# Two-layer graph block: low parts of the scores added behind the attention's trip through DRAM, and one PSUM bank of scores for even and one for odd graphs

## The reference, cut to what matters

```python
def layer(h, params):                       # two layers; h: 128 graphs x 128 nodes x 384
    u = einsum('bid,bjd->bij', h, h) / sqrt(D)
    a = softmax(u, axis=-1)
    delta = a * adjacency_matrix
    attn = delta / (sum(delta, axis=-1, keepdims=True) + 1e-10)
    hl, hs, hr = h @ wl.T + b_l, h @ ws.T + b_s, h @ wr.T + b_r
    ctx = (attn * upper) @ hl + diagonal(attn) * hs + (attn * lower) @ hr
    o = (ctx - mean(ctx)) / sqrt(var(ctx) + 1e-12) * g + beta
    return relu(o)
x = layernorm(x + layer(layer(x)))          # eps 1e-5, over the features
```

## Time and profile before

| | us |
|---|---|
| median of 3 runs (lowest, highest) | 1632.81 (1631.94, 1633.05) |
| the profiled execution's own time | 1631.82 |
| its span, first to last instruction | 1630.1 |
| PE busy / DVE busy / ACT busy / POOL busy | 1605.1 / 1398.9 / 1078.0 / 1212.5 |
| granted TensorE clock, mean | 0.997 |
| share of the 16 DMA engines | 43.3% |

### The profile page before, as it was taken

The page is one execution under the profiler, slowest core; times in us unless marked ns, Lnnn a source line. Parts: engine busy times, 40 slices in busy tenths (PEclk is TensorE's granted clock), DMA queues, the critical chain, the costliest instruction groups (busy, mean ns, idle before and its releaser), DMA issues.

```text
span 1630.1 us, 35740 instructions
## 1 busy us (share of the span) xinstructions
PE 1605.1 (98%) x9509; PEld 1597.9 (98%) x9509; DVE 1398.9 (86%) x4368; ACT 1078.0 (66%) x2835; POOL 1212.5 (74%) x1542
## 2 busy tenths in 40 slices
PE   8999999999999999999999999999999999999996
PEld 7899999999999999999999999999999999999995
DVE  7788888888888888888888888888888888888886
ACT  6566666666666666666666666666666666666654
POOL 5677777777777777777777777777777777777764
PEclk9999999999999999999999999999999999999998
DMA  5444444444444444444444444444444444444431
GB/s 175 102 110 107 114 114 107 111 107 116 107 114 111 110 107 113 114 107 112 107 115 106 114 112 110 109 110 115 107 114 109 112 106 114 114 108 111 108 93 45
DMA packets 463943, 179.17 MB, mean 110 GB/s; under 512 B 348592, under 2 KB 462896, under 8 KB 463920
## 3 DMA queue, kind: packets, MB, share of 16 engines
q1 hardware_dynamic: 463920, 178.91, 43.3%
HBM read 112.92 MB, written 65.86 MB: 110 GB/s over the span
## 4 chain that ended last, share of the span: by engine, by line
PE 92%; DMA 1%; DVE 1%; SPq 1%; POOL 1%; ACT 1%; issue 1%; DVEq 0%; POOLq 0%; ACTq 0%
PE p_proj L430 70%; PE p_gather L517 16%; PE p_score L424 5%; PE p_score L446 1%; DMA rows_mem<-rows_blocks 1%; SPq L366 1%; DMA attnT_whole<-attn_mem 1%; SPq L351 0%; POOL rstd L1173 0%; POOL attnT L1163 0%; DVE stats L623 0%; POOL attnT_split L1169 0%; DVE p_gather L646 0%; DVE p_gather L619 0%; DVE rows_blocks L725 0%
## 5 line engine op out<-in xcount | busy, mean ns | idle before, releaser
L430 PE MATMUL p_proj<-w,hT_layer 128*128 128x384 f32 x6912 | 1368.6, 339 | 0.9 <-DVE w L744 0.5
L430 PEld LDWEIGHTS p_proj<-w,hT_layer 128*128 128x128 f32 x6912 | 1162.5, 188 | 2.0 <-POOL w L1220 1.0
L281 POOL TENSOR_TENSOR proj_split<-proj,proj_split 128x768 fp32r<-128x768 f32 x253 | 467.6, 1848 | 182.3 <-ACT proj_split L943 181.9
L517 PE MATMUL p_gather<-proj_split,attnT_split 128*128 128x384 f32 x1536 | 309.3, 335 | 2.3 <-POOL attnT_split L1169 1.6
L1173 POOL TENSOR_TENSOR rstd<-veps,neg_half 128x1 f32<-128x1 f32 x384 | 206.8, 549 | 91.9 <-DVE veps L632 82.6
L517 PEld LDWEIGHTS p_gather<-proj_split,attnT_split 128*128 128x128 f32 x1536 | 269.9, 188 | 4.7 <-POOL attnT_split L1169 2.7
L943 ACT ACTIVATE proj_split<-proj 128x768 fp32r<-128x768 f32 x256 | 214.9, 839 | 84.7 <-DVE proj L688 83.7
L688 DVE TENSOR_TENSOR proj<-p_proj,bias_all 128x768 f32<-128x768 f32 x256 | 244.9, 957 | 12.9 <-PE p_proj L430 5.1
L1169 POOL TENSOR_TENSOR attnT_split<-attnT,attnT_split 128x256 fp32r<-128x256 f32 x256 | 190.3, 743 | 71.0 <-ACT attnT_split L934 70.9
L947 ACT ACTIVATE o<-y,nbias,rstd 128x384 f32<-128x384 f32 x128 | 90.7, 709 | 227.0 <-POOL nbias L1177 227.0
L424 PE MATMUL p_score<-hT_layer 128*128 128x256 f32 x768 | 216.6, 283 | 1.8 <-DVE rows L720 0.8
(11 more groups left out here) (59 smaller groups left out, 1598.3 us busy)
## 6 DMA issues: line engine op xcount, KB each, us to landing
xt_raw<-xT SPq DMA_DIRECT2D x128, 192.0 KB, 2.6
xn<-x SPq DMA_DIRECT2D x128, 192.0 KB, 2.4
out<-o SPq DMA_DIRECT2D x128, 192.0 KB, 2.0
rows_mem<-rows_blocks SPq DMA_DIRECT2D x124, 192.0 KB, 1.9
rowsT<-rows_mem SPq DMA_DIRECT2D x496, 48.0 KB, 2.4
adj_layer<-adj SPq DMA_DIRECT2D x256, 64.0 KB, 1.9
attn_mem<-attn_blocks SPq DMA_DIRECT2D x124, 128.0 KB, 1.7
attnT_whole<-attn_mem SPq DMA_DIRECT2D x496, 32.0 KB, 2.2
```

The lines of the kernel that those rows point to most:

```text
L281: op.tensor_tensor(proj_split[u][:, LO], proj[u][:, UP:LOW + 1, :], proj_split[u][:, HI].bitcast(F32), ALU.subtract).then_inc(s_proj_lo[k], 1)
L430: return nc.tensor.matmul(p_proj[:, which, 0:D], hT_of(k, b)[:, slot, st, c, :], w[:, k, which, mv, c, :], start=(n == 0), stop=(n == 8))
L517: last = nc.tensor.matmul(home(k, b)[:, 0:D], AT_split[u][:, st, side, :], proj_split[u][:, mv, side, :], start=(side == UP and n == 0), s ...
```

## The change: what it does

1. In the loop there is no cross matmul. Instead ACT copies L of both layers at once (`copy_cross`, one 128x256 instruction for the two 128x128 ones), DVE turns its 32x32 blocks (`turn_cross`, L768), and they travel in the same DMAs as the attention (128x512 stored for 128x256, four loads of 16 block rows for 8). POOL adds the returned L^T to L (`add_cross`, L1311), and DVE adds that sum in `scaled_scores`.
2. Scores must be there earlier: those of (layer 1, graph i+2) and (layer 2, graph i-2) are now made in the self term of layer 1 (`pair_slice`), and layer 2's are scaled one iteration later than before. `hT_layer1` gets four slots for two, and the input is loaded and split one iteration earlier.
3. The two score banks are now one for even and one for odd graphs, each with both layers' parts. `E` moves to SBUF, and the diagonal reads the SBUF identity; `ident_p` is gone.
4. The order on DVE, ACT, POOL and SP changes accordingly. Of the 256 cross matmuls 11 stay, in the fill and the close.

```diff
+        E = [sb(f"exps{k}", [P, N]) for k in (1, 2)]
...
-        p_score = [bank("p_score1", [P, 4, N]), bank("p_score2", [P, 4, N])]
-        E = [p_score[0][:, 2, :], p_score[1][:, 2, :]]
+        p_score = [bank("p_score_even", [P, 4, N]), bank("p_score_odd", [P, 4, N])]
         p_rows = bank("p_rows", [P, 4, N])
-        ident_p = [p_score[0][:, 3, :], p_score[1][:, 3, :]]
...
+                elif last == 4:
+                    sp.wait_ge(s_cross_blocks, i - 3)
+                else:
                     sp.wait_ge(s_attn_blocks[1], i - 2)
...
+            def pair_slice(b0, slot0, b1, slot1, n):
...
+                if b0 is not None and 2 <= n < 2 + C:
+                    step = score_step(0, b0, slot0, n - 2)
+                    if n == 1 + C:
+                        step.then_inc(s_parts[0], 1)
+                if n == 2 + C:
+                    done(pe, s_lo[1], b1)
+                if 2 + C <= n < 2 + 2 * C:
+                    step = score_step(1, b1, slot1, n - 2 - C)
+                    if n == 1 + 2 * C:
+                        step.then_inc(s_parts[1], 1)
...
-                    score0 = (0, i + 1, q) if live(i, i + 1) else None
-                    project_sides(0, i, p, 1, i - 4, range(18), score0)
-                    project_self(0, i, p, 1, i - 4)
+                    b0 = i + 2 if live(i, i + 2) else None
+                    project_sides(0, i, r, 1, i - 4, range(18))
+                    project_self(0, i, r, 1, i - 4, pair=(b0, (r + 2) % 4, i - 2, p))
                     gather(1, i - 4)
-                    project_sides(1, i - 3, q, 0, i, range(18), (1, i - 2, p))
+                    project_sides(1, i - 3, q, 0, i, range(18))
                     project_self(1, i - 3, q, 0, i)
                     gather(0, i)
...
+            def turn_cross(i, slot):
+
+
+                done(dve, s_crossed, i - 4)
+                if live(i, i + 2):
+                    nc.vector.transpose(blocks[:, slot, 2:4].rearrange("p k n -> p (k n)"),
+                                        crossed[:].rearrange("p k n -> p (k n)")).then_inc(s_cross_blocks, 1)
...
-                nc.vector.tensor_tensor_reduce(A[k][:], E[k], adj_tile[k][:, slot, :], 1.0, 0.0, ALU.mult,
+                nc.vector.tensor_tensor_reduce(A[k][:], E[k][:], adj_tile[k][:, slot, :], 1.0, 0.0, ALU.mult,
                                                ALU.add, col(k, b, slot, ADJSUM)).then_inc(s_attn[k], 1)
...
                 done(dve, s_attn[k], b)
-                nc.vector.tensor_tensor_reduce(diag_scratch[k][:], A[k][:], ident_p[k], 1.0, 0.0, ALU.mult,
+                nc.vector.tensor_tensor_reduce(diag_scratch[k][:], A[k][:], ident[:], 1.0, 0.0, ALU.mult,
...
                 normalise_layer1(i - 1, q)
                 low_rows(i - 2, p)
+                if not isinstance(i, int) or i > 4:
+                    done(dve, s_cross_sum, i - 5)
+                    output_mean(i - 5)
+                    if live(i, i + 1):
+                        scaled_scores(0, i + 1, q, cross_sum[:, 0])
+                    scaled_scores(1, i - 3, q, cross_sum[:, 1])
+                add_bias(0, i, True)
+                block_rows(i - 1)
                 mask(i, 1, i - 3, q)
                 if live(i, i + 1):
-                    done(dve, s_score[0], i + 1)
+                    mask(i, 0, i + 1, q)
                 diagonal(1, i - 3, q)
                 if live(i, i + 1):
-                    scaled_scores(0, i + 1, q)
-                add_bias(0, i, True)
-                block_rows(i - 1)
-                if live(i, i + 1):
-                    mask(i, 0, i + 1, q)
                     diagonal(0, i + 1, q)
+                turn_cross(i, p)
                 add_bias(0, i, False)
                 row_moments(1, i - 4, p)
                 row_variance(1, i - 4, p).then_inc(s_veps[1], 1)
                 centre_layer2(i, i - 4)
                 output_rows(i - 4, p)
-                done(dve, s_score[1], i - 2)
                 add_bias(1, i - 3, True)
-                scaled_scores(1, i - 2, p)
-                output_mean(i - 4)
                 add_bias(1, i - 3, False)
...
-                nc.scalar.activation(E[k], U[k][:], ACT.Exp, bias=col(k, b, slot, NEGMAX),
+                nc.scalar.activation(E[k][:], U[k][:], ACT.Exp, bias=col(k, b, slot, NEGMAX),
...
                 relu_rows(i, i - 2, p)
-                if live(i, i + 1):
-                    cross_scores(0, i + 1)
                 high_rows(i - 2, p)
-                high_sides(1, i - 4)
-                normalise_rows(i, i - 1)
                 if live(i, i + 1):
                     exponentials(0, i + 1, q)
+                exponentials(1, i - 3, q)
+                normalise_rows(i, i - 1)
+                high_sides(1, i - 4)
+                high_projections(0, i)
+                copy_cross(i, p)
                 high_sides(0, i)
-                high_projections(0, i)
-                if live(i, i + 2):
-                    high_input(i + 2, p)
+                if live(i, i + 3):
+                    high_input(i + 3, (r + 3) % 4)
                 if live(i, i + 1):
                     squared_denominators(0, i + 1, q)
                 squared_denominators(1, i - 3, q)
                 if live(i, i - 5):
                     output_squares(i - 5, q)
-                cross_scores(1, i - 2)
-                if live(i, i - 5):
                     finish(i, q)
                 high_projections(1, i - 3)
-                exponentials(1, i - 2, p)
...
+            def add_cross(first, last):
+                nc.gpsimd.tensor_tensor(cross_sum[:, first:last], crossed[:, first:last],
+                                        whole[:, 2 + first:2 + last], ALU.add).then_inc(s_cross_sum, 1)
...
                 low_projections(nc.gpsimd, pool, 1, i - 4)
                 attn_arrived(i - 1, q)
+                if not isinstance(i, int) or i > 4:
+                    add_cross(0, 2)
+                deviation_layer1(i - 1)
                 cut_sides(1, i - 4)
-                deviation_layer1(i - 1)
```

More of the change, by code:

```diff
@@ L183, in graph_block @@
         s_warm = sem("s_warm")
+        s_blank = sem("s_blank")
         def per_layer(name):
@@ L259, in attnT_count, with cross_count, swapped @@
             return b + 1 if k == 0 else b - G + 8
+        def cross_count(b):
+            return b + 1 if b < 6 else b - G + 6
         def rowsT_count(b):
             return b + 1 if b < 2 else b - G + 5
-        def attn_layers(i):
-            first = 0 if live(i, i + 1) and not direct(i, 0, i + 1) else 1
-            last = 2 if live(i, i - 3) and not direct(i, 1, i - 3) else 1
-            return first, last
+        def swapped(i):
+            return (1, 2) if isinstance(i, int) and i == G - 1 else (0, 4)
         def done_apart(eng, s, b):
@@ new lines, in load_swap @@
+            def load_swap(i, slot):
+                first, last = swapped(i)
+                sp.wait_ge(s_swap_out[slot], swap_moves(i, slot))
+                pieces = swap_mem[slot].rearrange("(r a) k (s b) -> s a k r b", a=B, b=B)
+                for s in range(4):
+                    rows_s = slice(s * B, (s + 1) * B)
+                    if last - first == 1:
+                        sp.dma_start(whole[rows_s, first, :].rearrange("a (r b) -> a r b", b=B),
+                                     pieces[s][:, first]).then_inc(s_swap_in[slot], 16)
+                    else:
+                        sp.dma_start(whole[rows_s, first:last, :].rearrange("a k (r b) -> a k r b", b=B),
+                                     pieces[s][:, first:last]).then_inc(s_swap_in[slot], 16)
@@ L423, in score_step @@
                 h = hT_of(k, b)
-                return nc.tensor.matmul(p_score[k][:, HI:LO + 1, :], h[:, slot, HI, n, :],
+                return nc.tensor.matmul(parts(k, slot), h[:, slot, HI, n, :],
                                         h[:, slot, HI:LO + 1, n, :], start=(n == 0), stop=(n == C - 1))
@@ L443, in score_slice @@
                 if n == last_part:
-                    done(pe, s_cross[k], b)
-                    nc.tensor.matmul(p_score[k][:, HI, :], cross[k][:], ident_r[:], start=False,
+                    pe.wait_ge(s_cross[k], cross_count(b))
+                    nc.tensor.matmul(parts(k, slot)[:, HI, :], cross[k][:], ident_r[:], start=False,
                                      stop=True, skip_group_check=True).then_inc(s_score[k], 1)
+            def pair_slice(b0, slot0, b1, slot1, n):
+                if n == 2:
+                    done(pe, s_negmax[1], b1 - 2)
+                    if b0 is not None:
+                        done(pe, s_lo[0], b0)
+                        done(pe, s_negmax[0], b0 - 2)
+                if b0 is not None and 2 <= n < 2 + C:
[8 more added lines that the diff above has]
+                        step.then_inc(s_parts[1], 1)
             def project_sides(k, b, slot, before, b_last, steps, scored=None, first=0, last_part=14):
```

242 lines of the change are left out of this document (138 added, 104 removed).

## The result

The changed kernel takes 1855.95 us (median of 4 runs, 1855.74 to 1856.24), the kernel before 1632.38 (4 runs): the ratio is 1.1371, with a 95% interval of 1.1351 to 1.1391. The prediction was 1926 us, slower, with a range of 1745 to 2160. Direction and mechanism came out as forecast; the size was 70 us too large, and one step was wrong, on the trip through DRAM.

The account below looks back on a forecast made before the run. PE bounds the kernel before; after the change a ring of waits through DVE, ACT and POOL does: 8.85 + 5.99 = 14.84 us, times 122 is 1810.5, with 113.3 outside and 1.7 around the span about 1926 us, range 1745 to 2160.

Parts of the forecast that it names:

- the removed matmuls: On PE, each cross matmul costs 0.11 us, two of them 0.22 an iteration; PE alone would need 12.24 us.
- From s to the turned rows: From s, DVE's first instruction waiting for POOL's `add_cross`, to the end of its turning: 4.60 us, with the lock 5.99.
- The lock: DVE's masks and diagonals, with two SBUF inputs, and POOL's instructions shut each other out: 1.39 us an iteration.
- R1: Rival: no lock on masks and diagonals, a ring of 13.45 us, 1756 us in all; chance 0.20.
- POOL's way: From the turning's end through layer 2's bias, POOL's low projections and `add_cross` to the next s: 8.85 us.
- The DRAM trip: Store, rows' loads, swapped loads, then `add_cross`, beside POOL's way: 8.2 us against 8.85, so not the longest way.
- the ring: One trip around the waits from s to the next s, no part overlapping itself: 14.84 us an iteration.
- R4: Rival: the swapped loads' issue or landing takes 2.5 us longer, 16.7 us an iteration, about 2150 us; chance 0.08.
- the 113.3 us outside the loop: Span outside the 122 iterations: 110.3 us as before, plus 3 for one more ring in the close and added scores.
- R2: Rival: POOL goes first at the diagonals, 16.7 us an iteration, 2150 us; chance 0.15 with its lucky side (1800).
- R3: Rival: the ring closes in time and PE hides everything, 12.24 us an iteration, 1606 us; chance 0.05.
- the sign named for the DRAM trip: POOL waiting for `whole` before `add_cross`, instead of going straight on, would show the DRAM trip is the longer way.

Follow-up runs that it names:

- experiment 3: The kernel before without any of its 256 cross matmuls, DVE waiting for ACT's copy instead: 1605.07 us (ratio 0.9847).
- e1_all_psum: The changed kernel with the diagonals' identity and the exponentials of the loop put back into PSUM: 1735.07 us (ratio 1.0639).
- e3_half_low: The changed kernel with POOL making the low part of layer 2's projections for only one triangle in the loop: 1838.82 us (ratio 1.1275).
- e12_orders_sbuf: e11_two_queues with exponentials and the diagonals' identity back in SBUF: 1808.61 us (ratio 1.109).
- e11_two_queues: e1_all_psum with ACT's and DVE's work reordered, and ACT issuing two of four rows' loads and two of four swapped loads: 1622.38 us (ratio 0.9941).
- e13_ident_orders: e12_orders_sbuf with the diagonals' identity alone read from PSUM: 1621.32 us (ratio 0.9951).
- e4_swap_first: The changed kernel with SP's four swapped loads (attention and low parts) issued ahead of the rows' loads: 2200.24 us (ratio 1.3491).

## Why the prediction was right, and where it was not

**What bounds it, and the removed matmuls.** Right: 0.10 to 0.11 us each (experiment 3) for 0.11.

**From s to the turned rows.** Forecast 5.99, measured 909.32 to 914.78, 5.46, and 5.43 to 5.47 in every iteration from 400 to 1300 us. The exponentials' chain to the turned rows took 1.93 (909.32 to 911.25) for 2.30: one exponential comes 0.40 after the other on ACT where I had taken 0.49, and ACT's first began 0.41 after s for 0.56, since DVE's mean holds the score back by 0.08 us and not by its 0.15. The lock, from 911.75 to 914.42, cost 2.67 - 1.44 = 1.23 for 1.39. The Trainium skill (SBUF — State Buffer, Who interferes with whom) says that a DVE instruction with two SBUF inputs contends with a GpSimd instruction that reads SBUF. The traces agree for the custom instruction as well, which the earlier trace rows could not show: its mask took 0.72 us here and 0.25 with one input in PSUM (e1_all_psum). Of the 1.23 us e1_all_psum gave back 0.99; its chain from s to the turned rows is 2.21 for 1.93 (904.17 to 906.38), with the wait for both scores in it. R1, no lock, was 1756; without the lock the kernel took 1735, 21 us less.

**POOL's way.** Forecast 8.85, measured 914.78 to 923.36, 8.58: 3.99 for 4.27 to the bias, 1.91 to POOL, 1.92 to the start of `add_cross`, 0.76 from there to s.

**The DRAM trip.** This step failed: "It is not the longest way", 8.2 against 8.85. Measured from the instruction behind the turning (900.27) to s (909.32) it took 9.05 in the iteration shown. In e3_half_low, where it alone closes the ring, it is 8.66 in the mean of the iterations from 400 to 1300 us (8.39 to 9.14). Store and rows' loads are as forecast (903.38 - 900.27 = 3.11 for 0.4 + 2.71). The swapped loads to POOL's start took 5.02 (903.38 to 908.40) for 4.27, and `add_cross` with its handover 0.92 for 0.81. I added nothing for the larger pieces because their issue would cost nothing more, which was nearly right (2.69 for four, 2.53 in the earlier trace rows), and forgot the landing: the page's median went from 2.2 us to 2.7. The line of the kernel before:

```profile
attnT_whole<-attn_mem SPq DMA_DIRECT2D x496, 32.0 KB, 2.2
```

In R4 I had this step at 2.5 us too much or nothing, and left out the 0.7 between, which was enough to make it tie.

**The sum.** POOL's way alone is 5.46 + 8.58 = 14.04, which is the distance of the two s shown; with the DRAM trip it is 5.46 + 9.05 = 14.51, the distance of the turnings at 899.91 and 914.42. POOL waited 13.0 us for `whole` in 56 iterations, 0.23 in the mean, and 14.04 + 0.23 = 14.27 for the forecast 14.84. The 14.27 takes the 113.3 us outside the loop from the prediction. By the 14.25 between the turnings in the trace, the iterations were 0.59 x 122 = 72 us too long in the forecast and the outside 2 us too short, 70 us in all. The overestimates (0.53 in the first half, 0.27 in the second) are partly given back by the trip that I had ruled out.

**Rivals.** R2 hung on 0.14 us and did not come here (0.10 us ahead, 913.49 against 913.59); in e12_orders_sbuf its mechanism did, at 1.5 us an iteration. That it stayed away here is luck: 0.10 us is less than the errors of the steps ahead of it. R3, that PE hides everything, needed the ring under 12.46; e11_two_queues and e13_ident_orders have that, by other orders and a second queue.

**What was to be seen.** DVE waits for `cross_sum` each iteration (0.92 and 0.52) and for the rows (0.46, forecast 0.5). POOL did wait for `whole`, the sign named for the DRAM trip. PE's idle time is mostly not where I put it: in front of layer 1's first projections it waits 0.27 us an iteration (15.0 in 56), in front of layer 2's gathers, for POOL's low triangles, 1.15 (64.6 in 56). PE's share is 89% and not 83%: 12.24 / 14.27 is 86%. The rest is in part how a record is drawn, since a matmul's lasts 0.34 us where the next starts 0.174 later, and each of the two stops leaves that tail; in part the matmuls are slower, 0.177 in the 27 projections from 913.60, and why is open.

## What to carry to other kernels

When an edit makes an engine wait for something that it feeds itself, add up that ring, every way round it, before counting what is saved: 27 us of matmuls bought a ring of 14.3 us in place of 12.46, and only all of it at once, no held instruction in the ring, two issue queues and reordered work, brought it under. Of a transfer ask issue and landing separately. An instruction that can be shut out by another engine is held for whatever that engine happens to run, and the kernel pays for it only where others wait for it. So take the operand out of reach (here one tile into PSUM) rather than read a price off an order that the edit will shift.

## What the runs showed of the hardware

- The custom DVE instruction of mask and diagonal took 0.25 to 0.27 us with two SBUF inputs when it was free, 0.46 to 0.82 beside POOL's 0.73 to 0.78 us instructions in the changed kernel, and 1.74 and 1.92 behind POOL's of 1.85 and 1.89 us. With one input in PSUM it stayed at 0.25 to 0.29, beside the same POOL instructions.
- Four loads took as long to issue on one queue with 16 block rows as with 12 (2.69 and 2.59 us). The median landing, as the pages of the runs with one queue have it, was 2.5 to 2.7 us with 16, 2.4 to 2.5 with 12 and 2.2 with 8. Issued by ACT beside SP, two at a time, the swapped loads landed in 3.1 and 2.7 us, and the ring was shorter all the same.
- In e4_swap_first, whose mean granted clock was 0.901, PE's clock fell in both iterations between 900 and 929 us. Windows of PE there: us, PE busy (instructions), granted clock, DMA share, GB/s.

```profile
911.00:913.00 2.00, 2.00 (x8) 0.50 0.20 77
...
915.00:917.00 2.00, 2.00 (x14) 1.00 0.56 89
```

  0.50 is the lower level, 1.2 GHz. The 27 projections from 911.35 took 5.79 us there; in the changed kernel they took 4.93. Before the clock fell, PE had waited 1.96 us ahead of a score matmul (906.38), and it waited 1.05 more ahead of the gathers at 909.27; in the following iteration it waits 0.81 and 1.74 us (923.58 and 926.47), and the clock is at 0.51 from 927 to 929. In the changed kernel PE waits twice as well, 0.25 us (905.26) and 1.45 us (912.45), and the clock stays at 1.00 from 905 to 923 us.
